# A decay attention stage with whole-group LayerNorms, packed value products and no filler matmuls

## What is computed

```
h   = layernorm(x)                       # eps 1e-5
low = causal_conv(h, conv_w, 5 taps) + conv_b
hid = ln_w * layernorm(low + sqrt_beta**2 * (h - low) + h) + ln_b   # eps 1e-12
q, k, v = hid @ q_w.T + q_b, ...         # 8 heads
s   = q k / sqrt(8), masked causally
p_  = softmax(s);  later = total(p_) - cumsum(p_)
d   = exp(-softplus(gamma) * sqrt(later * |i - j|)), at least 1e-5
p   = softmax(mask(s * d));  p[row 0] = 0
x  += (p v) @ out_w.T + out_b
```

## Time and profile before

| | us |
|---|---|
| Median of 3 runs | 3803.72 |
| Lowest and highest run | 3796.95, 3818.18 |
| Profiled execution, its own time | 3843.11 |
| Its span in the trace | 3841.3 |

### The profile page before, as it was taken

One profiled execution on the slowest core, in us unless ns is written; L12 is line 12 of the kernel. 1 busy time (PEld: TensorE's weight loads), 2 busy tenths in 40 slices (PEclk: granted clock), 3 DMA queues, 4 the chain that ended last, 5 costly groups with the idle time before them and its releaser, 6 DMA issues. The chain is left out here.

```text
span 3841.3 us, 64998 instructions
## 1 busy us (share of the span) xinstructions
PE 3600.5 (94%) x21447; PEld 2492.5 (65%) x21558; DVE 2351.2 (61%) x5341; ACT 1807.6 (47%) x3601; POOL 1340.4 (35%) x1395
## 2 busy tenths in 40 slices
PE   7996999999976999999999799999999999999766
PEld 6885676666653555555555467777777777777555
DVE  4694454444446544454445378888888878888643
ACT  2342333333332233233323167777777777777642
POOL 5460121111121000000000056666666666666461
PEclk9996798878787999999999689999999999999876
DMA  1110000000000000000000000000000000000002
GB/s 39 28 40 5 1 0 0 0 0 0 0 20 1 1 0 0 0 0 0 0 0 0 10 1 1 0 0 0 0 0 0 0 0 0 0 0 0 3 1 44
DMA packets 29609, 18.70 MB, mean 5 GB/s; under 512 B 23562, under 2 KB 26891, under 8 KB 29540
## 3 DMA queue, kind: packets, MB, share of 16 engines
q0 software_dynamic: 6144, 9.84, 1.1%
q1 hardware_dynamic: 23396, 7.99, 0.9%
HBM read 13.63 MB, written 4.19 MB: 5 GB/s over the span
## 5 line engine op out<-in xcount | busy, mean ns | idle before, releaser
L1285 DVE TENSOR_TENSOR prod<-c_h,act 128x512 f32<-128x512 f32 x352 | 243.5, 692 | 480.5 <-PE c_h L1137 396.5
L1217 ACT ACTIVATE act<-c_h 128x512 f32<-128x512 f32 x352 | 210.2, 597 | 655.8 <-PE c_h L1137 655.8
L1470 POOL TENSOR_TENSOR d_decay<-d_later,d_pos 128x512 f32<-128x512 f32 x256 | 326.1, 1274 | 478.8 <-DVE d_later L1887 478.8
L1164 PEld LDWEIGHTS c_out<-e_w,hid 128*128 128x128 f32 x2816 | 340.6, 191 | 79.5 <-issue 79.3
L1164 PE MATMUL c_out<-e_w,hid 128*128 128x64 f32 x2816 | 388.7, 281 | 0.1
L1887 DVE TENSOR_TENSOR_SCAN d_later<-d_cont,d_ex 128x512 f32<-128x512 f32 x256 | 314.2, 1228 | 49.7 <-ACT d_ex L1752 46.2
L1588 PEld LDWEIGHTS d_S<-d_kT,d_qT 8*128 8x128 f32 x2048 | 249.9, 188 | 110.9 <-issue 110.9
L1111 POOL TENSOR_TENSOR x_rest<-flatT,x_hm 64x512 f32<-64x512 bf16 (+1 forms) x33 | 38.2, 1157 | 748.8 <-ACT x_hm L1197 724.8
L1588 PE MATMUL d_S<-d_kT,d_qT 8*128 8x128 f32 x2048 | 299.1, 285 | 0.0
L1479 POOL TENSOR_TENSOR d_p<-d_p,d_mx 128x512 f32<-128x512 f32 x256 | 266.0, 1039 | 60.3 <-DVE d_mx L1906 59.0
L1582 PE MATMUL d_S<-d_hide,d_ident_b 128*128 128x512 bf16 x1088 | 283.1, 385 | 0.0
(11 more groups left out here) (320 smaller groups left out, 7412.6 us busy)
## 6 DMA issues: line engine op xcount, KB each, us to landing
out_h<-g_Y SPq DMA_DIRECT2D x8, 512.0 KB, 4.0
rows<-in_table,idx POOLq DMA_INDIRECT x128
e_w<-in_e_w SPq DMA_DIRECT2D x2, 704.0 KB
e_w<-in_e_w SPq DMA_DIRECT2D x1, 352.0 KB
d_pos<-in_d_pos SPq DMA_DIRECT2D x1, 256.0 KB
d_cont<-in_d_cont SPq DMA_DIRECT2D x1, 256.0 KB
g_w<-in_g_w SPq DMA_DIRECT2D x3, 64.0 KB, 2.1
d_win<-in_d_win SPq DMA_DIRECT2D x1, 146.2 KB
```

What stands on the lines that cost most here:

```text
L1164: last = nc.tensor.matmul(bo[:, b * D:(b + 1) * D], hid[u][:, b * P:(b + 1) * P], w2[:, c, :], start=(c == 0 and b == 0), stop=(c == NCH - ...
L1285: nc.vector.tensor_tensor(prod[u][:], b3[u][:], act1[u][:], ALU.mult).then_inc(S["multiplied"], 1)
L1470: pool.tensor_tensor(decay[u][:], later[u][:, 0:W], pos[:], ALU.mult).then_inc(S["placed"], 1)
```

## The change

Four things change, all in phase_decay_attention:

1. AGAIN is zero everywhere: the 34 filler matmuls per group are gone. The mask matmul that starts each score tile stays.
2. The value products of four heads are issued together, at every fourth step (k = 1 and 5 of 8), block by block, the four heads' column strips in turn: 16 matmuls at once where there were 4 times 4. To hold four transposed tiles until then, pT has 8 buffers where it had 4.
3. The first LayerNorm is made for the whole group at once: VectorE sums (128 x 4 out of 128 x 256), GpSimd scales the sums and subtracts the mean (d_hc), ScalarE squares, VectorE sums the squares, ScalarE makes 1/sqrt as before, GpSimd multiplies (d_xn).
4. The second LayerNorm loses its mean subtraction: the taps' mean over output features is taken out of the conv weights once, ahead of the loop (two VectorE instructions more there). ScalarE then squares out of PSUM, VectorE sums the squares, and one VectorE instruction multiplies.

The diff, cut to its core:

```diff
@@ -1315,7 +1315,7 @@
 
-    AGAIN = (4, 6, 6, 3, 3, 3, 3, 6)
+    AGAIN = (0,) * 8
     LAG_SCAN, LAG_DECAY, LAG_WEIGH, LAG_EXP2, LAG_TURN, LAG_PV, LAG_KEEP, LAG_Y = 1, 2, 3, 4, 5, 6, 7, 8
...
@@ -1356,7 +1358,7 @@
         ex, later, decay = slots("d_ex", [P, W]), slots("d_later", [P, 1 + W]), slots("d_decay", [P, W])
-        p2, pT = slots("d_p2", [P, W]), slots("d_pT", [P, W])
+        p2, pT = slots("d_p2", [P, W]), [m.sb(f"d_pT{u}", [P, W]) for u in range(2 * SLOTS)]
         rtot, inv = slots("d_rtot", [P, GB]), m.sb("d_inv", [P, GB, QUAD])
...
@@ -1448,6 +1452,22 @@
                 class Work(Beside):
+                    def norm(self, n, j):
+                        if j == 1:
+                            pool.wait_ge(G["summed"], G.now(n))
+                            pool.wait_ge(G["scaled"], G.before(n))
+                            pool.sem_inc(passed, 1)
+                            pool.tensor_scalar(mean[:], mean[:], 1.0 / D, None, ALU.mult).then_inc(G["mean_made"], 1)
+                            pool.wait_ge(G["mean_made"], G.now(n))
+                            pool.sem_inc(passed, 1)
+                            pool.tensor_tensor(hc[:], H[:, bass.ds(n * GB, GB), :], over(mean[:], D), ALU.subtract)\
+                                .then_inc(G["centred"], 1)
+                        if j == 5:
+                            pool.wait_ge(G["rstd_made"], G.now(n))
+                            pool.wait_ge(G["x_turned"], G.before(n))
+                            pool.sem_inc(passed, 1)
+                            pool.tensor_tensor(xn[:], hc[:], over(rstd[:], D), ALU.mult).then_inc(G["scaled"], 1)
+
                     def project(self, n, s, j):
...
@@ -1601,20 +1621,21 @@
                     on, q, u = unit(LAG_PV)
-                    if on:
-                        j = k - LAG_PV
+                    if on and (k - LAG_PV) % QUAD == QUAD - 1:
+                        j = k - LAG_PV - (QUAD - 1)
                         s, h = (j // GQ) % 2, j % GQ
...
                             pe.wait_ge(G["v_kept"], G.now(group_of(i, k, LAG_PV)))
-                        if h % QUAD == 0:
-
-                            pe.wait_ge(Q["attT_kept"], Q.before(quad_of(i, k + QUAD - 1, LAG_PV)))
+
+                        pe.wait_ge(Q["attT_kept"], Q.before(quad_of(i, k, LAG_PV)))
                         pe.wait_ge(S["pT_kept"], S.now(q))
-                        r = slice(h % QUAD * STRIP, (h % QUAD + 1) * STRIP)
                         for b in range(GB):
-                            last = nc.tensor.matmul(bO[r, b * P:(b + 1) * P], v[s][:, b, h, :],
-                                                    pT[u][:, b * P:(b + 1) * P], start=True, stop=True)
-                        last.then_inc(S["attended"], 1)
+                            for e in range(QUAD):
+                                last = nc.tensor.matmul(bO[e * STRIP:(e + 1) * STRIP, b * P:(b + 1) * P],
+                                                        v[s][:, b, h + e, :],
+                                                        pT[(j + e) % (2 * SLOTS)][:, b * P:(b + 1) * P],
+                                                        start=True, stop=True)
+                        last.then_inc(S["attended"], QUAD)
                     beside(i, k, work)
...
@@ -1649,7 +1670,18 @@
 
+                    def norm(self, n, j):
+                        if j == 3:
+                            act.wait_ge(G["centred"], G.now(n))
+                            act.wait_ge(G["spread"], G.before(n))
+                            nc.scalar.activation(sq[:], hc[:], ACT.Square).then_inc(G["squared"], 1)
+
                     def filter(self, n, j):
+                        if j == 7:
+                            act.wait_ge(G["filtered"], G.now(n))
+                            act.wait_ge(G["spread2"], G.before(n))
+                            nc.scalar.activation(sq2[:], grouped(bX1[:, 0:GB * D], D), ACT.Square)\
+                                .then_inc(G["squared2"], 1)
                         if j == 3:
...
@@ -1739,8 +1772,10 @@
                         act.wait_ge(S["turned"], S.now(q2))
-                        act.wait_ge(S["attended"], S.past(q2))
-                        nc.scalar.activation(pT[u2][:], bT[:], ACT.Copy).then_inc(S["pT_kept"], 1)
+                        if not (isinstance(q2, int) and q2 < 2 * SLOTS):
+                            act.wait_ge(S["attended"], S.ago(q2, 2 * SLOTS))
+                        nc.scalar.activation(pT[(k - LAG_TURN) % (2 * SLOTS)][:], bT[:], ACT.Copy)\
+                            .then_inc(S["pT_kept"], 1)
                     if on:
...
@@ -1780,6 +1815,8 @@
                 link(nc.vector.tensor_tensor(conv[0:D, TAPS - 1, :], conv[0:D, TAPS - 1, :], diag[:], ALU.add))
+                link(nc.vector.tensor_reduce(tapsum[:], conv[:], AX, ALU.add))
+                link(nc.vector.scalar_tensor_tensor(conv[:], over(tapsum[:], D), -1.0 / D, conv[:], ALU.mult, ALU.add))
                 dve.wait_ge(fold, 1)
...
@@ -1809,47 +1846,27 @@
                     def norm(self, n, j):
+                        if j == 0:
+                            dve.wait_ge(G["centred"], G.before(n))
+                            nc.vector.tensor_reduce(mean[:], H[:, bass.ds(n * GB, GB), :], AX, ALU.add)\
+                                .then_inc(G["summed"], 1)
                         if j == 3:
-                            dve.wait_ge(G["centred"], G.before(n))
-                            for b in range(GB):
-                                last = nc.vector.bn_stats(
-                                    st[:, b, :], H[:, bass.ds(n * GB + b, 1), :].rearrange("p b d -> p (b d)"))
-                            last.then_inc(G["stats"], 1)
-                            dve.wait_ge(G["stats"], G.now(n))
-                            dve.sem_inc(passed, 1)
-                            for b in range(GB):
-                                last = nc.vector.bn_aggr(mv[:, b, :], st[:, b, :])
-                            last.then_inc(G["moments"], 1)
-                        if j == 5:
-                            dve.wait_ge(G["rstd_made"], G.now(n))
-                            dve.wait_ge(G["x_turned"], G.before(n))
-                            for b in range(GB):
-                                last = nc.vector.tensor_scalar(
-                                    xn[:, b, :], H[:, bass.ds(n * GB + b, 1), :].rearrange("p b d -> p (b d)"),
-                                    mv[:, b, 0:1], rstd[:, b:b + 1], ALU.subtract, ALU.mult)
-                            last.then_inc(G["centred"], 1)
+                            dve.wait_ge(G["squared"], G.now(n))
+                            dve.wait_ge(G["rstd_made"], G.before(n))
+                            nc.vector.tensor_reduce(ss[:], sq[:], AX, ALU.add).then_inc(G["spread"], 1)
 
...
                         if j == 7:
-                            dve.wait_ge(G["filtered"], G.now(n))
-                            dve.wait_ge(G["centred2"], G.before(n))
-                            for b in range(GB):
-                                last = nc.vector.bn_stats(st2[:, b, :], bX1[:, b * D:(b + 1) * D])
-                            last.then_inc(G["stats2"], 1)
-                            dve.wait_ge(G["stats2"], G.now(n))
-                            dve.sem_inc(passed, 1)
-                            for b in range(GB):
-                                last = nc.vector.bn_aggr(mv2[:, b, :], st2[:, b, :])
-                            last.then_inc(G["moments2"], 1)
+                            dve.wait_ge(G["squared2"], G.now(n))
+                            dve.wait_ge(G["rstd2_made"], G.before(n))
+                            nc.vector.tensor_reduce(ss2[:], sq2[:], AX, ALU.add).then_inc(G["spread2"], 1)
 
...
                             dve.wait_ge(G["h_turned"], G.before(n))
-                            for b in range(GB):
-                                last = nc.vector.tensor_scalar(hn[:, b, :], bX1[:, b * D:(b + 1) * D], mv2[:, b, 0:1],
-                                                               rstd2[:, b:b + 1], ALU.subtract, ALU.mult)
-                            last.then_inc(G["centred2"], 1)
+                            nc.vector.tensor_tensor(hn[:], grouped(bX1[:, 0:GB * D], D), over(rstd2[:], D), ALU.mult)\
+                                .then_inc(G["scaled2"], 1)
 
```

More of the change, by code:

```diff
@@ L1339, in phase_decay_attention @@
         notfirst = m.sb("d_notfirst", [P, 1])
-        st, mv, rstd = m.sb("d_st", [P, GB, 6]), m.sb("d_mv", [P, GB, 2]), m.sb("d_rstd", [P, GB])
-        st2, mv2, rstd2 = m.sb("d_st2", [P, GB, 6]), m.sb("d_mv2", [P, GB, 2]), m.sb("d_rstd2", [P, GB])
+        mean, ss, rstd = m.sb("d_mean", [P, GB]), m.sb("d_ss", [P, GB]), m.sb("d_rstd", [P, GB])
+        ss2, rstd2 = m.sb("d_ss2", [P, GB]), m.sb("d_rstd2", [P, GB])
+        hc, sq, sq2 = m.sb("d_hc", [P, GB, D]), m.sb("d_sq", [P, GB, D]), m.sb("d_sq2", [P, GB, D])
+        tapsum = m.sb("d_tapsum", [KX, TAPS])
```

(23 more changed lines are left out.)

## The result

The changed kernel takes 4045.2 us (median of 4 runs, 4030.0 to 4064.5) beside 3806.7 us for the kernel before in the same comparison. The ratio is 1.063, 95% interval 1.057 to 1.068: slower, where 3675 us was forecast. The second rival happened.

The account below looks back on a forecast made before the run. PE was taken to bound the decay loop at 44.03 us per group; 30.8 us of work at clock 0.77 makes 40.0, saving 129 us over 32 groups: 3803.7 - 129 = 3675 us, range 3560 to 3910.

Parts of the forecast that it names:

- The second rival: Decay loop: PE waits for VectorE, loses clock, then binds at 1.83 times; 3911 us at clock 0.65; chance 0.22.
- I take 0.77, a little below the mean of the two stages that show both levels: Decay loop's mean clock, from block attention's 0.85 and another stage's 0.78; gives 40.0 us per group.
- a gain of 5.9 us: PE time per group saved by packed value products if four strips run side by side; 1.1 if not.
- The strips run side by side: Packed value products: 32 records within 1.0 to 1.2 us at full clock, against 3.4 one after another.
- The low level's factor: PE work at half clock takes 1.83 times as long as at full clock, from ten conv records.
- PE's 30.8 us per group at full clock: Decay loop: PE's 44.03 us per group less 7.4 for fillers and 5.9 for packed value products.
- Between them PE binds with 30.8 / clock: Decay loop's group time between full and always half clock; 40.0 us at clock 0.77.
- The rival's turning point: Mean loop clock where 30.8 / clock equals the old 44.03 us group: 0.70, below which the change is slower.
- The likeliest case: The forecast with PE binding the decay loop at clock 0.82 to 0.72: 3610 to 3740 us, chance 0.40.
- The LayerNorms: Decay loop: VectorE sheds short instructions, about 2.5 us per group; GpSimd reaches 28.5; worth nothing under PE's 44 us.
- VectorE's loop of 36.5 us: Decay loop: VectorE's least time per group, 4.51 us a unit plus divisions, binding if the clock stays full.

Follow-up runs that it names:

- e2: Kernel before with all 34 fillers per group taken out and nothing else changed: ratio 1.020.
- f2: Kernel before with only the packed value products (four strips side by side) and their 8 pT buffers; old LayerNorms and 34 fillers kept: ratio 1.062.
- e1: Changed kernel with the 34 fillers per group back in front of the scores: 4069.0 us, ratio 1.058.
- e3: Changed kernel with 34 fillers per group back, each reading 32 rows instead of 128: 4628.7 us, ratio 1.21, one run.
- f3: Changed kernel with 34 fillers back plus 14 dense matmuls per group behind the turn transposes of steps 0, 3, 4 and 7: 3762.6 us, ratio 0.985.
- g1: Changed kernel with 48 fillers per group, all in front of the scores, the extra 14 at steps 1 and 2: 4035.0 us, ratio 1.054.
- h1: Kernel before with four heads' value products batched but issued head by head, no strips side by side; old LayerNorms, 34 fillers: 3982.5 us, ratio 1.048.
- f1: Changed kernel with value products by head and 34 fillers back, leaving only the LayerNorm edit: ratio 0.997.
- h2: Kernel before with four heads' value products batched, two strips side by side at a time; old LayerNorms, 34 fillers: ratio 1.070.
- e4: Changed kernel with 13 fillers per group at chosen steps instead of none: 4124.7 us, ratio 1.077.
- g2: Kernel before with 19 fillers per group instead of 34 and nothing else changed: 3761.4 us, ratio 0.982.
- g4: Kernel before with the new LayerNorms and 19 fillers per group instead of 34, value products by head: 3756.5 us, ratio 0.982.

## Why the prediction was wrong

**The step that failed** is "I take 0.77, a little below the mean of the two stages that show both levels". The loop ran at 0.57. The two stages suit the loop as far as the fillers go: e2, which only drops them, had 0.82. They were no measure of a loop with packed value products. What the runs showed in its place: the packing alone takes the clock from 1.00 to 0.71 and gives the whole slowdown, 6.2% (f2). The clock moved with the number of rows that the fillers use (e1 0.72, e3 0.52), with where in the group they stand (f3 0.99, g1 0.80), and with the value products batched instead of head by head (kernel before 1.00, h1 0.83). The prediction listed the packing under time, a gain of 5.9 us, and gave its effect on the clock half a sentence; what would be lost it put down mainly to the fillers. By themselves the fillers' removal costs 2.0% (e2) and the packing 6.2% (f2); together they cost 6.3%, not the sum of 8.2%.

**Steps that held.** The strips run side by side: 1.01 us for 32 records at full clock, as forecast. That the number came out so well is luck, for two errors cancel: head by head the 32 records take 2.39 us (h1) and not 3.4, and side by side they take 2.4 times less and not 3.4 times. The low level's factor: 2.00 / 1.08 = 1.85 for the scores, 1.83 predicted. PE's 30.8 us per group at full clock (its own terms give 30.7) agree with an estimate from the new trace: a mean clock of 0.57 between the levels 0.5 and 1 puts 86% of the time on the low one, 43.7 of the 50.8 us per group, and leaves 7.1 on the full one, so 43.7 / 1.83 + 7.1 = 31.0. Of the second rival the sign and the second half of the mechanism: PE is the bound at the low level, and VectorE waits for its scores. Its first half, that PE waits for VectorE and loses the clock by that, isn't in the trace: PE never waited for VectorE in the 1200 us, and e3's clock was the lowest with 0.03 us of idle time.

**A term that was mis-sized.** "Between them PE binds with 30.8 / clock" is too steep, since the low level costs 1.83 and not 2: at 0.57 it gives 54.0 us a group, and 50.8 were measured. With 86% of the time on the low level and 30.8 / (1 - 0.86 x (1 - 1 / 1.83)) it is 50.5. The rival's turning point moves from a mean clock of 0.70 to 0.67. The likeliest case was also added up wrongly: by the prediction's own formula a clock of 0.82 to 0.72 gives 3597 to 3764 us, not 3610 to 3740.

**The LayerNorms.** Predicted as worth nothing while PE needs 44 us per group, and f1 shows it: 1409 us in both. VectorE's part of a group goes from 36.0 to 34.1 us (928 / 1200 x 44.03), 1.9 less where 2.5 was said; GpSimd's is 29.3 where 28.5 was said.

**VectorE's loop of 36.5 us** was reached by no run: the best group, f3's, took 42.0 us (1343 / 32) with PE busy for 1189 of 1200 us.

**The rule of the Trainium skill.** PE was busy for 1195 of 1200 us at 0.57, and for all of 1200 at 0.52 in e3. By the Trainium skill (TensorE: Matmul & The Clock Gate, Part 1) the clock is lost in idle stretches; this trace doesn't agree, since no idle stretch is there to carry the loss. What the Trainium skill (TensorE: Matmul & The Clock Gate, Part 4) says of transposes, that they don't count as PE work for the clock, is not tested by any of these runs; it pointed to the low end, near which the clock came out, but the experiments put most of the loss on the value products, which are no transposes.

## What to carry to other kernels

Here a batch that PE does faster cost more by the clock than it gave in time (h1, h2, f2). So price both, and undo each edit alone before blaming the obvious one. Where a loop at full clock loses all-row matmuls from some of its steps, try filler work in those steps, and not only where it is easy to add (f3 against g1). A filler that fails to bring the clock back costs double, so a half measure can be worse than none (e4). And a filler table that once held the clock can be too long: with the products by head, 19 kept the clock as 34 did, and the kernel took 1.8% less (g2, g4).

## What the runs showed of the hardware that was not expected

- PE recorded busy throughout, at 0.52 with fillers on 32 rows: 1199.97 of 1200 us in e3.
- Value products batched but issued head by head: 32 records in 2.39 us, against 3.96 in four pieces of eight, and 3.4 as the prediction's 0.10 us a record had it. Why they cost less isn't shown.
- VectorE's scan grew when GpSimd got the LayerNorm products, and more when the loop ran faster. Mean of one is the last number ahead of the second bar's idle time, before and then g4:

```profile
L1887 DVE TENSOR_TENSOR_SCAN d_later<-d_cont,d_ex 128x512 f32<-128x512 f32 x218 | 267.2, 1226 | 41.6 <-ACT d_ex L1752 38.3 <-issue 3.3
```

```profile
L1903 DVE TENSOR_TENSOR_SCAN d_later<-d_cont,d_ex 128x512 f32<-128x512 f32 x229 | 329.2, 1437 | 81.9 <-ACT d_ex L1786 80.7
```

1.23 us against 1.44, with GpSimd busy for 742 and 860 of 1200 us. With the new LayerNorms and 34 fillers (f1) it is 1.27 us, with the old ones and 19 fillers (g2) 1.26. No run separates what causes it.
